# Transformer block in split half precision: two tiles of batch 0 normalised on another engine, one row of idle products out, the hand-written order changed at both ends

## What is computed

```python
def attn(t, W_qkv, b_qkv):                       # D = 256
    Q, K, V = split(t @ W_qkv.T + b_qkv)
    attn = softmax(Q @ K.T / sqrt(256))
    return attn @ V
def ffn(x, w_gate, w_up, w_down):                # integer weights / 127, hidden 768
    return (silu(x @ wg.T) * (x @ wu.T)) @ wd.T
x = t                                            # (16, 1024, 256) float32
x = x + layernorm(attn(layernorm(x)))
x = x + layernorm(ffn(layernorm(x)))
```

## Time and profile before

| what | us |
|---|---|
| median of 3 runs (1334.54 to 1337.27) | 1334.54 |
| the profiled execution, its own time | 1335.11 |
| its span, first to last instruction | 1333.2 |
| PE busy in it | 1311.1 |
| DVE, ACT, POOL busy | 953.6, 1020.0, 993.3 |
| idle time of PE between 0 and 20 | 5.1 |
| idle time of PE between 80 and 120 | 3.8 |
| idle time of PE between 200 and 1000 | 1.7 |
| idle time of PE between 1300 and the end | 7.8 |

### The profile page before, as it was taken

How to read it: one execution, slowest core, us unless ns; L and a number is a source line. 1 busy time by engine, 2 the same in 40 slices (tenths; PEclk the granted TensorE clock), 3 DMA queues, 4 the chain that set the end, 5 groups by cost and what they waited for, 6 DMA issues and landing times.

```text
span 1333.2 us, 23133 instructions
## 1 busy us (share of the span) xinstructions
PE 1311.1 (98%) x7210; PEld 705.2 (53%) x7210; DVE 953.6 (72%) x2670; ACT 1020.0 (77%) x1610; POOL 993.3 (75%) x1081
## 2 busy tenths in 40 slices
PE   8999999999999999999999999999999999999997
PEld 4444455554555555555554555545555554555554
DVE  7786676776868768677686767767687686866565
ACT  6767687887877778787887878878777887877645
POOL 4687487786877868688796877868778686875744
PEclk9999999999999999999999999999999999999999
DMA  6997648665776865579666876666668655846622
GB/s 191 173 164 139 130 82 166 127 136 118 119 142 128 156 119 114 119 135 174 119 111 123 133 150 127 131 128 114 143 127 160 120 110 118 149 106 127 107 61 65
DMA packets 492111, 171.98 MB, mean 129 GB/s; under 512 B 473041, under 2 KB 475473, under 8 KB 491986
## 3 DMA queue, kind: packets, MB, share of 16 engines
q1 hardware_dynamic: 491184, 169.67, 65.0%
q10 hardware_dynamic: 802, 0.79, 0.2%
HBM read 36.70 MB, written 16.78 MB: 40 GB/s over the span
## 4 chain that ended last, share of the span: by engine, by line
PE 43%; POOL 2%; SPq 1%; issue 1%; DMA 1%; DVE 1%; ACT 1%; POOLq 0%; ACTq 0%; DVEq 0%
PE S L1073 35%; PE S L1232 8%; DMA yTl<-yl 1%; POOL Pl L449 1%; SPq L309 1%; SPq L278 0%; POOL yl L476 0%; POOL qTl L426 0%; POOL rs L364 0%; DMA PTh<-Ph 0%; DVE X L986 0%; SPq L315 0%; ACT xh L558 0%; ACT P L614 0%; ACT yn L634 0%
## 5 line engine op out<-in xcount | busy, mean ns | idle before, releaser
L449 POOL TENSOR_TENSOR Pl<-P,Ph 128x1024 f16<-128x1024 f32 x128 | 272.9, 2143 | 72.3 <-issue 41.2
L1073 PE MATMUL S<-PTh,xh 128*128 128x512 f16 x512 | 194.1, 379 | 0.0
L1073 PE MATMUL S<-PTl,xh 128*128 128x512 f16 x512 | 194.0, 379 | 0.0
L1073 PE MATMUL S<-PTh,xl 128*128 128x512 f16 x512 | 194.0, 379 | 0.0
L651 ACT ACTIVATE hf<-S,sc 128x512 f32<-128x512 f32 x192 | 129.4, 683 | 65.1 <-PE S L1073 55.4
L1073 PE MATMUL S<-Wh,hTh 128*128 128x256 f16 x768 | 170.3, 273 | 0.3 <-DVE X L986 0.2
L1073 PE MATMUL S<-Wh,hTl 128*128 128x256 f16 x768 | 170.3, 273 | 0.0
L614 ACT ACTIVATE P<-P,nmx,sc 128x1024 f32<-128x1024 f32 x112 | 138.1, 1233 | 36.3 <-DVE nmx L901 36.1
L485 POOL TENSOR_TENSOR hTl<-hf,hTh 128x512 f16<-128x512 f32 x128 | 146.8, 1156 | 18.8 <-ACT hTh L658 17.1
L364 POOL TENSOR_TENSOR rs<-rs,mhalf 128x4 f32<-128x4 f32 (+2 forms) x160 | 144.6, 903 | 13.3
L1073 PE MATMUL S<-yTh,Gh 128*128 128x512 f16 x384 | 146.1, 381 | 4.5 <-DMA yTl<-yl 4.4
(11 more groups left out here) (206 smaller groups left out, 3248.9 us busy)
## 6 DMA issues: line engine op xcount, KB each, us to landing
xs<-in_L_attn_t SPq DMA_DIRECT2D x32, 512.0 KB, 4.6
X<-in_L_attn_t SPq DMA_DIRECT2D x32, 512.0 KB, 4.6
out_x<-X SPq DMA_DIRECT2D x62, 256.0 KB, 2.8
PTh<-Ph SPq DMA_TRANSPOSE x128, 3.8
PTl<-Pl SPq DMA_TRANSPOSE x128, 3.4
hTl<-in_L_ffn_w_gate SPq DMA_DIRECT2D x1, 768.0 KB, 8.1
hTh<-in_L_ffn_w_up SPq DMA_DIRECT2D x1, 768.0 KB, 9.8
hTl<-in_L_ffn_w_down SPq DMA_DIRECT2D x1, 768.0 KB, 11.1
```

Of the source, the lines that this page charges most:

```text
L449: p.engine.tensor_tensor(out=Pl[:, m % 3, :], in0=P[:, m % 4, :], in1=Ph[:, m % 3, :], op=ALU.subtract).then_inc(pl_vector if i in PL_ON_V ...
L1073: done = t.engine.matmul(out, s, m, start=(start and i == 0), stop=(stop and i == len(terms) - 1))
```

## The change

- `X0_ON_SCALAR` becomes (0, 1, 4, 5, 6, 7) and `X0_ON_VECTOR` (2, 3): DVE normalises tiles 2 and 3 of batch 0 ahead of `bound`, and ACT tiles 4 and 5.
- ACT takes tiles 0, 1, 4, 5, then `xT_first_high(a, 0, 4, 0)`, `A_high`, `xT_first_high(a, 0, 4, 1)`, and only then tiles 6 and 7 and `x_high(a, 0, 0)`.
- The second `keep_busy`, of 6 products, goes.
- SP issues the loads of the second and third feed-forward weights ahead of the second x load of batch 1, and the first weights after it.
- The lists of all five engines are in another order in the start (to about the first third of batch 3) and in the end (from the first attention of batch 14). The loop of 12 passes is the same, and so are all helpers.

```diff
-X0_ON_SCALAR = (0, 1, 2, 3, 6, 7)
-X0_ON_VECTOR = (4, 5)
+X0_ON_SCALAR = (0, 1, 4, 5, 6, 7)
+X0_ON_VECTOR = (2, 3)
...
             c_product(t)
-            keep_busy(t, 6, const_done, 3, 0)
             first_z(t, 0, 2, 0)
...
             row_sizes(v)
+            x_first_vector(v, 2)
+            x_first_vector(v, 3)
             bound(v)
             scale_A(v)
-            x_first_vector(v, 4, 5)
+            c_scales(v)
             xT_first_low(v, 0, 4, 0)
             A_low(v)
             xT_first_low(v, 0, 4, 1)
             x_stats(v, 1, 0)
-            c_scales(v)
-            x_stats(v, 1, 1)
             z_float(v, 0, 0, 2)
...
             x_low(p, 2, 1)
             mix_keys(p, 2)
+            y_low(p, 0, 0)
             y_norm(p, 0, 1)
-            t_low(p, 2, 0)
-            y_low(p, 0, 0)
...
             load_x(s, 1, 0)
+            load_ffn(s, 1)
+            load_ffn(s, 2)
             load_x(s, 1, 1)
             load_ffn(s, 0)
-            load_ffn(s, 1)
-            load_ffn(s, 2)
...
             z_part(t, 2, 0, 0, 6, (ol_done[0], 2))
+            gate_up(t, 0, 0, 0, 0, (exp_done, 15), (exp_done, 15), three)
             z_part(t, 2, 0, 1, 7, (ol_done[1], 2))
-            gate_up(t, 0, 0, 0, 0, (exp_done, 15), (exp_done, 15), three)
...
             gate_up(t, 15, 1, 2, 2, (silu_done, 186), (hl_vector, 62), three)
+            down(t, 15, 0, 1, (ft_done[1], 60), three)
+            down(t, 15, 0, 0, (ft_done[0], 60), three)
             gate_up(t, 15, 1, 3, 6, (silu_done, 187), (hmul_done, 187), three)
-            down(t, 15, 0, 0, (ft_done[0], 60), three)
             gate_up(t, 15, 1, 4, 0, (silu_done, 188), (hmul_done, 188), three)
             gate_up(t, 15, 1, 5, 2, (silu_done, 189), (hl_vector, 63), three)
-            down(t, 15, 0, 1, (ft_done[1], 60), three)
             last_down(t, three)
```

More of the change, by code:

```diff
@@ L1551, in _ @@
             p_low(p, 0, 3)
+            x_low(p, 0, 1)
+            x_norm(p, 2, 0)
+            x_low(p, 1, 1)
+            z_low(p, 1, 0)
             p_low(p, 0, 4)
-            z_low(p, 1, 0)
-            x_norm(p, 2, 0)
             p_low(p, 0, 5)
@@ L1579, in _ @@
             h_low(p, 0, 0, 4)
-            x_low(p, 3, 0)
-            t_low(p, 2, 1)
+            p_low(p, 1, 4)
+            q_low(p, 2, 0)
+            x_norm(p, 3, 0)
             h_low(p, 0, 1, 0)
             h_low(p, 0, 1, 1)
-            q_low(p, 2, 0)
+            d_norm(p, 0, 0, 0)
+            t_low(p, 2, 1)
             p_low(p, 1, 5)
             p_low(p, 1, 6)
+            d_norm(p, 0, 0, 1)
+            x_low(p, 3, 0)
             p_low(p, 1, 7)
-            d_norm(p, 0, 0, 1)
-            d_norm(p, 0, 0, 0)
             p_low(p, 2, 0)
             q_low(p, 2, 1)
+            h_low(p, 0, 1, 3)
+            x_norm(p, 3, 1)
             p_low(p, 2, 1)
-            x_norm(p, 3, 1)
             y_norm(p, 1, 0)
@@ L1652, in _ @@
             h_low(p, 13, 1, 1)
+            p_low(p, 14, 4)
             d_norm(p, 13, 0, 0)
-            p_low(p, 14, 4)
+            d_norm(p, 13, 0, 1)
             p_low(p, 14, 5)
-            d_norm(p, 13, 0, 1)
+            h_low(p, 13, 1, 3)
             p_low(p, 14, 6)
+            h_low(p, 13, 1, 4)
             p_low(p, 14, 7)
-            q_low(p, 15, 1)
-            h_low(p, 13, 1, 3)
             p_low(p, 15, 0)
             p_low(p, 15, 1)
-            h_low(p, 13, 1, 4)
+            q_low(p, 15, 1)
             y_norm(p, 14, 0)
+            x1_norm(p, 14, 0)
             p_low(p, 15, 2)
-            x1_norm(p, 14, 0)
+            y_low(p, 14, 0)
             p_low(p, 15, 3)
-            y_low(p, 14, 0)
+            p_low(p, 15, 4)
             y_norm(p, 14, 1)
+            d_norm(p, 13, 1, 0)
             x1_norm(p, 14, 1)
@@ L1686, in _ @@
             x1_norm(p, 15, 0)
+            h_low(p, 14, 1, 0)
+            y_low(p, 15, 0)
             h_low(p, 14, 1, 1)
-            y_low(p, 15, 0)
             y_norm(p, 15, 1)
@@ L1838, in _ @@
             y_high(a, 1, 0)
+            exp(a, 2, 4)
             copy_m1(a, 2, 3)
+            p_high(a, 2, 4)
             x_high(a, 3, 1)
@@ L1842, in _ @@
             copy_u3(a, 2, 3)
-            exp(a, 2, 4)
             exp(a, 2, 5)
@@ L1993, in _ @@
             copy_u3(a, 15, 3)
+            exp(a, 15, 6)
+            p_high(a, 15, 5)
+            p_high(a, 15, 6)
             silu(a, 14, 0, 0, 6)
             silu(a, 14, 0, 1, 0)
-            p_high(a, 15, 4)
-            p_high(a, 15, 5)
+            silu(a, 14, 0, 2, 2)
             h_high(a, 14, 0, 0)
             h_high(a, 14, 0, 1)
-            silu(a, 14, 0, 2, 2)
+            h_high(a, 14, 0, 2, 2)
+            y_hat(a, 14, 1, 0)
             silu(a, 14, 0, 3, 6)
-            exp(a, 15, 6)
@@ L2014, in _ @@
-            silu(a, 14, 0, 5, 2)
+            add_bias(a, 13, 1, 1)
+            o_high(a, 15, 0, 0)
             silu(a, 14, 1, 0, 0)
-            h_high(a, 14, 0, 5, 2)
+            add_bias(a, 14, 0, 1)
+            o_high(a, 15, 1, 0)
+            add_bias(a, 14, 0, 0)
             h_high(a, 14, 1, 0)
-            add_bias(a, 13, 1, 0)
-            add_bias(a, 14, 0, 0)
-            o_high(a, 15, 0, 0)
+            o_high(a, 15, 1, 1)
+            y_hat(a, 15, 0, 0)
+            y_hat(a, 15, 0, 1)
@@ L2021, in _ @@
             silu(a, 14, 1, 1, 2)
-            add_bias(a, 13, 1, 1)
-            add_bias(a, 14, 0, 1)
+            silu(a, 14, 1, 2, 0)
+            y_high(a, 15, 0)
             h_high(a, 14, 1, 1)
-            silu(a, 14, 1, 2, 0)
-            o_high(a, 15, 1, 1)
+            h_high(a, 14, 1, 2, 0)
             silu(a, 14, 1, 3, 2)
-            y_hat(a, 15, 0, 0)
-            o_high(a, 15, 1, 0)
-            y_hat(a, 15, 0, 1)
-            y_high(a, 15, 0)
-            h_high(a, 14, 1, 2, 0)
@@ L2039, in _ @@
             silu(a, 15, 0, 1, 0)
-            h_high(a, 15, 0, 0)
+            silu(a, 15, 0, 2, 2)
             y_hat(a, 15, 1, 0)
@@ L2559, in second_part @@
             pair_second(t, 15, 2)
+            attend_part(t, 14, 1, 3)
+            pair_third(t, 15, 2)
+            attend_part(t, 14, 1, 5)
+            attend_part(t, 14, 1, 6)
             attend_part(t, 14, 1, 7)
-            pair_third(t, 15, 2)
-            attend_part(t, 14, 1, 2)
-            attend_part(t, 14, 1, 1)
-            attend_part(t, 14, 1, 3)
             pair_last(t, 15, 2)
@@ L2571, in second_part @@
             gate_up(t, 14, 0, 1, 0, (u3_copied, 56), (c11_done, 56), three)
+            down(t, 13, 1, 0, (x1_done, 118), three)
             pair_last(t, 15, 3)
-            down(t, 13, 1, 0, (x1_done, 118), three)
             down(t, 13, 1, 1, (x1_done, 120), three)
```

576 lines of the change are left out of this document (287 added, 289 removed).

## The result

The changed kernel takes **1322.57 us** (median; 1322.07 to 1323.97) against 1334.54 before (1333.95 to 1337.27): a ratio of 0.9914, 95% interval 0.9900 to 0.9929. Its profiled execution took 1322.73, of which 1320.9 are the span. I had forecast 1327.5 with 1325.6 as the lower end: right in sign and in most places, but the gain is 12.0 and not 7.0. A measurement of the kernel before had a spread of 3.3 us here and of 6.9 over the later comparisons; the changed one stays within 2.4 over all twelve of its own.

The account below looks back on a forecast made before the run. PE was taken as the bound, busy 1311.1 of a 1333.2 us span. The terms 2.0 + 0.9 + 2.4 + 1.7 - 1.0 + 1.0 = 7.0 off the median 1334.54 gave 1327.5, range 1325.6 to 1331.5.

Parts of the forecast that it names:

- The first 22 us: Start up to group 1's first_z: reordered ACT, DVE and loads start it at 19.6 instead of 21.70; gain 2.0 us.
- Whether it reaches 90 us: From the start to 90 us: POOL's new order might use up the gain; 0.2 us charged, 0.9 with a slow landing.
- score(1,7): PE's wait for exp(1,5), between 85 and 105 us: of 1.20 us about 0.25 stays; gain 0.9.
- gate_up(0,0,0): PE's 2.52 us yTl wait near 100 us: earlier y_low leaves 0.1, gain 2.4; low clock behind it goes, gain 1.7.
- What is late next: After gate_up(0,0,0), up to the loop: ACT late for gate_up c=4 and z_part(2,1,0); loss 1.0 us (0.3 to 2.0).
- The loop: The 12 unchanged passes: the loop is the old one, with the same idle time; counted as 0.
- (e): Rival, slower: POOL handed over later, each of 12 loop passes waits 0.6 to 0.9 us more for yTl, up to 1338; 6%.
- The end: Last batches, up to the last product: gate_up(15,1,0) starts earlier as its chain moves 1.0 earlier; gain 1.0 us (0.5 to 1.6).
- (a): Rival: the clock falls in the first 20 us without the idle products, costing 1.7 us, giving 1329.2; 15%.
- (b): Rival: the start's 2 us are used up at attend(0,0) and score(1,0) by POOL's longer line, giving 1329.5; 15%.
- (c): Rival: the yTl wait is only halved, 1.2 us left, and the clock falls anyway, giving 1330.4 to 1331.5; 10%.
- (d): Rival: the change doesn't act, PE meets the loop's first DMA waits at the same time, 1332 to 1334.5; 8%.

Follow-up runs that it names:

- its own experiment: Changed kernel with c_scales put back behind VectorE's low halves and x_stats(1,0): 1323.09 us in one execution, beside 1322.46 for the changed kernel.
- the front alone: Kernel before with everything of the change ahead of the loop, and the old end: 1326.05 us beside 1334.19, ratio 0.9943.
- the start alone: Kernel before with only the change of the first 22 us, POOL's list as before: 1333.89 us beside 1334.19, ratio 1.0004.

## Why the forecast was right, and where it fell short

1322.57 lies 3.0 below the lower end of the range. In the terms of the sum, three steps failed: the loop, put at nothing because "the loop is the old one", gave 1.92; the end, 1.0 with a bound of 1.6, gave 2.39; and "what follows the last product is unchanged" gave 0.79. The other terms together came to 7.3 where 6.0 were forecast. One by one:

- **The first 22 us** (2.0; 2.38). Right, step by step: Ah and xTh, c_scales (1.0 by its own experiment), x_stats(1,1) behind zw. (My bounds there were loose: by the same steps a landing of 6.2 would leave a gain of 1.1 and not 1.4.) The load took 4.55 to land, so my middle value of 5.2 was pessimistic by 0.65. By my reading of the ring order in the Trainium skill (DMA: Bandwidth & Descriptors, Queues, rings and completion order) the weights behind it would not delay it at all. In the fourteen profiles of the new order it landed after 4.3 to 4.9, in the six of the old, with no weights close behind, after 3.6 to 4.0, so the traces don't bear that reading out; what they show lies about half-way between it and my 5.2. What I missed is the other side of that step. In the kernel before, group 1's first_z hung on the landing of the second load, and that varies: the wait was 0.95 in the profile I read, 0.20, 0.58, 1.84 and 2.18 in others and none in the sixth, as that load took 5.4 to 7.2 us to land. With the new order it is 0.00 in all fourteen profiles. One execution had told me the term's size but not that it is a variable one.
- **Whether it reaches 90 us** (-0.2; 0). Right, but only by POOL's x_norm(1,0) ahead of the x_low and ACT's z_high(0,1) ahead of x_hat(1,1). I had looked at POOL's new list as a risk alone; without it and ACT's the start's gain is gone.
- **score(1,7)** (0.9; 0.90, rest 0.30 for 0.25). Right.
- **gate_up(0,0,0)** (2.4 and 1.7; 4.38 together). The size was right for this profile and the cause too narrow: y_low moved alone makes the kernel slower. I listed load_x(3,0)'s place nowhere, though it is a DMA that the moved transpose had to pass. The clock's echo came in three of seven profiles with the wait; that the profile I read was one of them, and so the 1.7 came true, is luck.
- **What is late next** (-1.0; -0.37). Wrong in size. The wait at gate_up c=4 (0.35) didn't come, by 0.06; that at z_part(2,1,0) was 0.15 for 0.65. The transpose landed 3.0 after issue and not 3.9, and PE never waited for it, so ACT's seven steps began 0.35 earlier.
- **The loop** (0; 1.92). The first step that failed: "the loop is the old one". Its code is; its waits are not, and I had looked at them for a loss alone, in (e). From profile to profile the loop's gain is 1.4 to 2.5, so the 1.92 is one draw of it. In the pair of the ledger 1.29 of it is idle time (eight waits against three) and the rest goes with the overlap of the five waits fewer. Through what, beyond the row's wait at batch 6, the new front shortens the loop, is not shown.
- **The idle row** (0; about 1.6 in the medians). "The 6 idle products lay in PE's wait and cost nothing" is true of PE's time at 13 us and wrong for the kernel.
- **The end** (1.0; 2.39). The waits for `oTl` and at gate_up(15,1,0) went as forecast, and 0.42 came at down for 0.55. Mis-sized was the chain to the last group, the second step that failed: project_v(15,1) starts 2.8 earlier and not 0.9, because gate_up(14,1,3) no longer stands ahead of it. The chain follows with 1.9 (x1_add, y_hat and y_low alike), its transposes land 0.6 sooner, and the wait of 0.45 vanishes instead of setting the pace. A further 0.5 is again the overlap that waits hide.
- **Behind the last product** (0; 0.79). The third step that failed, of open cause (above). The landing spread over 0.6 in the old end and 0.9 in the new, so part of it is chance.
- **Rivals.** (a), a low clock in the first 20 us, does occur: in two of the twelve profiles of the new front without the row, at 1.4 us each, not as a rule. This is PE's granted clock in one of them, the front alone (length, busy, clock, DMA):

```profile
12.00:13.00 1.00, 0.49 (x5) 1.00 0.81 209
13.00:14.00 1.00, 0.99 (x3) 0.59 0.81 240
14.00:15.00 1.00, 1.00 (x5) 0.50 0.87 258
15.00:16.00 1.00, 1.00 (x6) 0.50 1.02 327
16.00:17.00 1.00, 1.00 (x6) 0.70 1.09 398
```

  Its kernel was 8.1 us faster than before all the same. The Trainium skill (TensorE: Matmul & The Clock Gate, Part 4: PE-mode transpose) says that a transpose does not count as busy in the same way, and by that rule this case would be likely. The transposes are the same in all twelve, and only two have it. (b) didn't occur in the changed kernel, but it is what the start alone ran into, with POOL's old list in place of its new one. (c) and (d) didn't occur. (e) had the right organ: the loop's chain to yTl has almost no spare and is sensitive to what the start hands over. I gave it the wrong sign.

The range failed since its bounds covered only terms that had a number. Even its best case for those, 8.9, was passed by the 9.7 that they gave, and the terms without a number, which could have come out either way, added 2.7.

## What to carry to other kernels

A step moved on one engine earns only what the queue that issues its DMA allows: before moving it, read what stands ahead of its transfer, and what that waits for. Waits in a loop of equal passes can belong to the program, and removing instructions far away can move them; take more profiles before calling them noise, or calling them fixed: here one of 0.45 stood in two profiles of a program and not in the third. And price a wait at its idle time plus the overlap that it breaks (0.16 here).
